# Near keys per block of 64 queries instead of 128, in an attention kernel on one NeuronCore

## The chip, the cores and the metric

The kernel runs on one core of a Trainium2 chip. The metric is the device time of one execution in microseconds; the numbers below are the median of three runs and one profiled execution. The engines are PE (TensorE, matmuls; PEld is its loading of weights), DVE (VectorE), ACT (ScalarE), POOL (GpSimd) and SP (SyncE, which here only issues DMAs).

## The reference

`x` is [4, 2048, 256] in float32. It is normalised over its last axis (xn), and the result is x plus an attention of xn plus a linear layer of xn with weights and activations rounded to fp8. The attention has 16 heads of 16 columns and a sparse mask:

```python
def _strided_allowed(S):                       # STRIDE = 4, LOCAL = 8
    i = jnp.arange(S)[:, None]
    j = jnp.arange(S)[None, :]
    return (j % STRIDE == 0) | (jnp.abs(i - j) <= LOCAL)
...
q = q * jax.nn.sigmoid(unity_scale)
scores = jnp.einsum('bhqd,bhkd->bhqk', q, k) / jnp.sqrt(jnp.asarray(D, x.dtype))
scores = jnp.where(allowed, scores, -jnp.inf)
attn = jax.nn.softmax(scores, axis=-1)
out = jnp.einsum('bhqk,bhkd->bhqd', attn, v)
out = out.transpose(0, 2, 1, 3).reshape(B, S, H)
return out @ o_w + o_b
```

So each query sees every fourth key of the sequence (512 "far" keys, the same for all queries) and the keys within 8 places of it ("near" keys, of which only those not divisible by 4 are still missing).

## The kernel before, in words

The first part (part_project) normalises x, computes q, k, v and the linear layer, splits q and k into parts in float16 and writes q, k, v to DRAM. The change touches it only where v is written: `v_sb` has 17 columns a head, the last of them 1, which gives the sum of the softmax.

The second part (part_attend) has 64 steps: 4 batches x 4 groups of 4 heads (16 iterations) x 4 blocks of 512 queries. The four heads of a group are two pairs (p = 0, 1); the two heads of a pair (f = 0, 1) lie in the two halves of the partitions of `q_op` and `k_op`, 48 rows each (51 with the negated maximum), so that the two matmuls of a pair can run side by side in two halves of the array's rows.

Each step does three things, and each for another step of the sequence:

- Maxima. For the next step and the one after it, PE computes the scores with queries in the partitions (`unit`): eight far units (128 queries x 512 far keys x 2 heads, L1105) and two near units (two tiles of 128 queries each, 108 near keys a tile: a mask matmul L1116 and the products L1123). Each unit fills one of two buffers of two PSUM banks (`ps_u`), and one DVE reduction (L1012, L1015) empties it. When the maxima of a step are complete, DVE joins them (L995, `maximum`, after AHEAD = 5 units), POOL splits the result into three parts in bf16 (L819 to L825), PE transposes it (L1061, `score_peaks`), ACT copies it (L946) and SP copies it into three rows of `q_op` (L859), where the far and near scores of the next step subtract it.
- Scores of the step itself, with keys in the partitions: `score_far` (L1070, 128 far keys x 512 queries, two heads, two banks; 8 pairs a step) and `score_near` (a mask matmul L1080 and a product L1083 for each tile of 128 queries, 108 keys a tile; 2 pairs of banks a step). ACT takes the exponential of each bank (L953 far, L958 near) into `probs`. There are three banks for scores (`ps_s`); `free_score` waits for the entry three before.
- The weighing (`weigh`): four rounds of far keys (L1142, four heads in four quarters of the array's columns, f32, 512 queries) and one of near keys (L1149, the same in tiles of 128 queries), all into one bank `ps_o`. ACT copies it out (L937) after the last round; DVE inverts the sums (L988), POOL multiplies (L810), SP stores.

Each engine's order is written out by hand. PE's is in `body(st)` of `tensor_attend`, ACT's in SCORE_PAIRS, DVE's in MAXIMA. PE's step before is:

```python
far_unit(2, 1); far(0, 0); weigh_last(2); far(0, 1); far_unit(1, 0); far_unit(0, 0)
far(2, 1); weigh_last(3); far(1, 0); near_unit(0); far_unit(2, 0); far(1, 1)
weigh_last(4); near(0); far_unit(3, 1); far_unit(1, 1); far(2, 0); weigh_own(0)
maxima(); far(3, 1); far_unit(3, 0); near_unit(1); far(3, 0); weigh_own(1)
near(1); far_unit(0, 1)
```

SP's order in a step: the shares of the step before to DRAM (L883), q of three steps ahead (L100), one piece of the next iteration's k or v (`load_piece` 0), the shares back, broadcast (L895), the attention rows out (L899), the sums (L851), the second piece (`load_piece` 1), the negmax rows (L859). The pieces of places 0 and 1 are k, those of places 2 and 3 are v: one DMA of far v (`r` = -1) and three of near v (L844, 36 rows x 16 tiles of 272 bytes each).

A third part multiplies with `o_w` and adds (L1222, L1031).

Of the kernel before, what the change touches and what calls it, by code (L numbers as in the profile page):

```python
# [22 lines left out]
BF16 = mybir.dt.bfloat16  # L23
F16 = mybir.dt.float16
I32 = mybir.dt.int32
ALU = mybir.AluOpType
# [19 lines left out]
HALF = P // 2  # L46
# [4 lines left out]
MASK_K = WPAD + S - NS + WPAD  # L51
# [7 lines left out]
VR = D + 1  # L59
EPS = 1e-5  # L60
BANDS = ((1, 18), (6, 6), (21, 5))
# [41 lines left out]
def part_project(nc, io, dram, keep, ctx):  # L103

    with ExitStack() as memory:
# [31 lines left out]
        v_sb = sb("v_sb", [P, 2, TT, NH, VR])  # L137
# [72 lines left out]
        def sync_project(sp):  # L210
# [13 lines left out]
            sp.dma_start(keep["mask_k"][:], io["near_k"].bitcast(BF16)).then_inc(keep["bands_loaded"], 16)  # L224
            sp.dma_start(keep["mask_q"][:], io["near_q"].bitcast(BF16)).then_inc(keep["bands_loaded"], 16)
# [53 lines left out]
        def gpsimd_project(pool):  # L279
# [5 lines left out]
            nc.gpsimd.memset(v_sb[:, 0, :, :, D:VR], 1.0).then_inc(v_set, 1)  # L285
            nc.gpsimd.memset(v_sb[:, 1, :, :, D:VR], 1.0).then_inc(v_set, 1)
# [23 lines left out]
        def scalar_project(act):  # L310
# [6 lines left out]
            def body(j, n):  # L317
# [27 lines left out]
                if main:  # L345
# [7 lines left out]
                    if not (isinstance(c, int) and c < 2):  # L353
                        act.wait_ge(v_stored[k], 16 * earlier(j, n))
                    nc.scalar.activation(
                        v_sb[:, k].rearrange("p t h w -> p (t h) w")[:, :, 0:D],
                        ps_v.rearrange("p a (t w) -> p (a t) w", w=D), ACT.Copy).then_inc(v_copied, 1)
# [267 lines left out]
UNITS = TT * PAIRS + TT // 2  # L625
# [3 lines left out]
AHEAD = 5  # L629
# [5 lines left out]
    ("near", 0), ("far", 2, 0), ("negmax",), ("far", 3, 1), ("far", 3, 0),  # L635
    ("near", 1),
# [3 lines left out]
    ("far", 2, 1), ("far", 1, 0), ("far", 0, 0), ("near", 0), ("far", 2, 0),  # L640
    ("far", 3, 1), ("far", 1, 1), ("far", 3, 0), ("near", 1), ("far", 0, 1),
# [17 lines left out]
def part_attend(nc, io, dram, keep, out, ctx, done):  # L659
# [69 lines left out]
    k_op, mask_k, mask_q = keep["k_op"], keep["mask_k"], keep["mask_q"]  # L729
    v_op = [keep["v_op"], sb("v_op1", [P, NS // P + S // P, HG * VR])]  # L730
    probs = sb("probs", [P, ROUNDS, HG, CH])
# [53 lines left out]
    def window(p, tile):  # L785
        return p * S + WSTEP * tile
# [3 lines left out]

    def close(tile):
        return WSTEP * tile
# [39 lines left out]
    def sync_attend(sp):  # L832
        def load_v(it, par, windows=range(-1, STRIDE - 1)):

            v = dram["v"][it // G, :, it % G * HG * VR:(it % G + 1) * HG * VR]
            for r in windows:
                if r < 0:
                    to, src = v_op[par][:, 0:NS // P, :], v[LOCAL:LOCAL + S, :].rearrange(
                        "(c p r) w -> r p c w", p=P, r=STRIDE)[0]
                else:  # L840
# [73 lines left out]
        for k in range(2):  # L914
            sp.wait_ge(done["qk_stored"][k], 16 * 12 * B * CPB // 2)
            sp.wait_ge(done["v_stored"][k], 16 * B * CPB // 2)
        load_v(0, 0)
# [11 lines left out]
    def scalar_attend(act):  # L929
# [9 lines left out]
        def body(st):  # L939
            todo = st.entries()  # L940
            for kind in todo:
# [12 lines left out]
                else:  # L954
                    h = kind[1]
                    if kind in OPENS and st.n >= 1:
                        act.wait_ge(pv_done, ROUNDS * st.at())
                    ins = nc.scalar.activation(probs[0:WIN, ROUNDS - 1, h], ps_s[st.bank(kind)][0:WIN], ACT.Exp,  # L958
                                               scale=undo)
# [19 lines left out]
    def vector_attend(dve):  # L979

        def body(st):
# [16 lines left out]
            for i, kind in enumerate(MAXIMA):  # L998
# [14 lines left out]
                else:  # L1013
                    tile = 2 * kind[1]
                    ins = nc.vector.tensor_reduce(peak_near[:, :, tile:tile + 2].rearrange("q f t p -> q f (t p)"),  # L1015
                                                  banks[:, :, 0:2 * PAIRS * WIN].rearrange("q f (g w) -> q f g w",
                                                                                           w=WIN), AX_X, ALU.max)
# [26 lines left out]
    def tensor_attend(pe):  # L1044
# [27 lines left out]
        def score_near(st, p):  # L1072

            q, k = q_op[:, st.slot()], k_op[st.parity()]
            banks = [free_score(st, ("near", 2 * p + f)) for f in range(2)]
            for t in range(TT):
                tile = st.queries() * TT + t
                cols, at, at_mask = slice(t * P, (t + 1) * P), window(p, tile), close(tile)
                for f in range(2):
                    nc.tensor.matmul(banks[f][0:WIN, cols], mask_k[half(f), at_mask:at_mask + WIN],  # L1080
                                     mask_q[half(f), tile * P:(tile + 1) * P], start=True, stop=False)
                for f in range(2):
                    ins = nc.tensor.matmul(banks[f][0:WIN, cols], k[half(f, KM), at:at + WIN], q[half(f, KM), p, cols],  # L1083
                                           start=False, stop=True)
                    if t == TT - 1:
                        ins.then_inc(s_ready, 1)

        def unit(st, kind):
# [21 lines left out]
            for t in range(2):  # L1110
                tile = 2 * kind[1] + t
                cols = slice(tile * P, (tile + 1) * P)
# [248 lines left out]
```

## Time and profile before

| | |
|---|---|
| median of three runs | 1126.22 us (1123.71 to 1129.16) |
| span of the profiled execution | 1127.2 us, mean granted clock 0.986 |
| PE busy | 1070.1 us (95%) |
| DVE busy | 948.4 us (84%) |
| ACT busy | 811.9 us (72%) |
| POOL busy | 248.4 us (22%) |
| largest groups | L1012 DVE 608.7 us, L953 ACT 541.4 us, L1142 PE 270.2 us, L1070 PE 254.2 us, L1105 PE 187.9 us |

Busy time of an engine is the union of its instructions' intervals; matmuls overlap, and their ends are modelled, so PE's share is not its load. The rows of a timeline merge neighbouring instructions of one line: the first number is the start of the first, the second the time to the end of the last, and xN their count. The first 237 us or so are the projections, the last 60 us the output matmuls; between them lie the 64 steps.

### The profile page before, as it was taken

Reading aid. Unit: us, or ns where it says so; the run is one execution under the profiler, and the core shown is the slowest. Engines: PE = TensorE matmul, PEld = TensorE weight load, DVE = VectorE, ACT = ScalarE, POOL = GpSimd, SP = SyncE. Lnnn points to the kernel's source line nnn. Section 1 sums busy time; section 2 is a strip of 40 time slices with the busy share of each in tenths; the row PEclk is TensorE's granted clock in tenths of the full one; section 3 lists DMA queues with packets and bytes.
Section 4 is the critical chain, followed back from the end, with each engine's and each line's share of the span. In section 5 each row is a group of like instructions: output and inputs, shape, how many; then the busy total and the mean of one; then the engine's idle time right before and its main releaser. Section 6 shows DMA issues by size and latency. Waiting matters only on the chain.

```text
span 1127.2 us, 28640 instructions
## 1 busy us (share of the span) xinstructions
PE 1070.1 (95%) x10945; PEld 484.3 (43%) x10945; DVE 948.4 (84%) x1203; ACT 811.9 (72%) x1524; POOL 248.4 (22%) x381
## 2 busy tenths in 40 slices
PE   5899999969999999999999999999999999999898
PEld 3566666623333333333333333333333333333387
DVE  5888877588999999999999999999898999999133
ACT  2444344327988898888888888888898888888700
POOL 1433333301121212212121212212121212222100
PEclk9999999968999999999999999999999999999999
DMA  6566666641232333333332333333333333231167
GB/s 188 184 197 206 206 209 209 196 111 44 81 87 81 99 91 85 87 103 104 95 107 82 112 91 105 89 96 111 94 99 93 99 94 94 86 84 48 55 216 246
DMA packets 167066, 134.21 MB, mean 119 GB/s; under 512 B 70652, under 2 KB 146172, under 8 KB 166924
## 3 DMA queue, kind: packets, MB, share of 16 engines
q1 hardware_dynamic: 164344, 128.19, 38.4%
q10 hardware_dynamic: 2592, 4.26, 1.1%
q8 instruction: 85, 1.39, 0.5%
q14 instruction: 45, 0.37, 0.1%
HBM read 71.26 MB, written 59.84 MB: 116 GB/s over the span
## 4 chain that ended last, share of the span: by engine, by line
PE 74%; DVE 12%; issue 7%; DMA 5%; ACT 2%; SPq 0%; DVEq 0%; ACTq 0%
PE ps_attend L1142 15%; PE ps_attend L1070 11%; DVE peak_far L1012 10%; PE ps_attend L1105 9%; PE ps_attend L1149 5%; PE ps_attend L1222 5%; PE ps_project L607 5%; PE ps_project L597 5%; PE ps_project L576 4%; PE ps_attend L1080 4%; DMA sums<-out_rows 3%; PE ps_attend L1116 3%; PE ps_project L540 2%; PE ps_attend L1083 2%; PE ps_attend L1123 2%
## 5 line engine op out<-in xcount | busy, mean ns | idle before, releaser
L1012 DVE TENSOR_REDUCE peak_far<-ps_attend 128x2 f32<-128x1024 f32 x512 | 608.7, 1221 | 42.7 <-PE ps_attend L1105 31.3
L953 ACT ACTIVATE probs<-ps_attend 128x512 f32<-128x512 f32 x1024 | 541.4, 598 | 49.4 <-PE ps_attend L1070 46.2
L1142 PE MATMUL ps_attend<-probs,v_op 128*17 128x512 f32 x2048 | 270.2, 600 | 0.0
L1070 PE MATMUL ps_attend<-q_op,k_op 51*128 51x512 f16 x1024 | 254.2, 387 | 4.9 <-ACT probs L953 3.3
L1105 PE MATMUL ps_attend<-k_op,q_op 48*128 48x512 f16 x1024 | 187.9, 388 | 25.7 <-DVE peak_far L1012 15.3
L958 ACT ACTIVATE probs<-ps_attend 108x512 f32<-108x512 f32 x256 | 138.9, 594 | 35.7 <-PE ps_attend L1083 35.7
L1070 PEld LDWEIGHTS ps_attend<-q_op,k_op 51*128 51x128 f16 x1024 | 76.8, 93 | 195.6 <-ACT probs L953 137.4
L819 POOL CAST negmax<-peak 128x16 bf16<-128x16 f32 x64 | 12.7, 198 | 612.8 <-DVE peak L995 612.8
L1015 DVE TENSOR_REDUCE peak_near<-ps_attend 128x8 f32<-128x864 f32 x128 | 131.0, 1023 | 10.5 <-PE ps_attend L1123 10.4
L810 POOL TENSOR_TENSOR out_rows<-out_rows,share_rows 128x512 f32<-128x512 f32 x64 | 81.4, 1272 | 65.4 <-DMA share_rows<-shares_dram 63.0
L1105 PEld LDWEIGHTS ps_attend<-k_op,q_op 48*128 48x128 f16 x1024 | 49.7, 94 | 98.6 <-DVE peak_far L1012 71.6
L1080 PEld LDWEIGHTS ps_attend<-mask_q,mask_k 48*108 48x108 bf16 x1024 | 60.0, 125 | 69.4 <-ACT probs L953 56.1
L1080 PE MATMUL ps_attend<-mask_q,mask_k 48*108 48x128 bf16 x1024 | 78.7, 228 | 0.8 <-ACT probs L953 0.8
L1083 PE MATMUL ps_attend<-q_op,k_op 51*108 51x128 f16 x1024 | 73.6, 218 | 0.0
L1149 PE MATMUL ps_attend<-probs,v_op 108*17 108x128 f32 x2048 | 68.3, 274 | 0.0
L328 ACT ACTIVATE qk_parts<-ps_project,ranges 128x1024 f16<-128x1024 f32 x16 | 17.8, 1114 | 68.6 <-PE ps_project L576 62.0
L297 POOL TENSOR_TENSOR quant<-quant,power 128x1024 f32<-128x1024 f32 x16 | 37.7, 2357 | 116.9 <-DVE qk_parts L436 80.3
L1116 PE MATMUL ps_attend<-mask_k,mask_q 48*128 48x216 bf16 x512 | 59.0, 260 | 4.1 <-DVE peak_far L1012 1.6
L1083 PEld LDWEIGHTS ps_attend<-q_op,k_op 51*108 51x108 f16 x1024 | 61.5, 126 | 0.0
L576 PE MATMUL ps_project<-xnT,wq 128*128 128x512 f32 x128 | 60.2, 614 | 1.2 <-ACT xnT L335 1.2
L1142 PEld LDWEIGHTS ps_attend<-probs,v_op 128*17 128x17 f32 x2048 | 34.0, 95 | 59.3 <-issue 58.6
L1123 PE MATMUL ps_attend<-k_op,q_op 48*128 48x108 f16 x1024 | 58.4, 210 | 0.0
(82 smaller groups left out, 1037.9 us busy)
## 6 DMA issues: line engine op xcount, KB each, us to landing
share_rows<-shares_dram SPq DMA_DIRECT2D x64, 256.0 KB
attn_dram<-out_rows SPq DMA_DIRECT2D x64, 256.0 KB, 5.5
q_dram<-qk_parts SPq DMA_DIRECT2D x96, 128.0 KB
k_dram<-qk_parts SPq DMA_DIRECT2D x96, 128.0 KB
q_op<-q_dram SPq DMA_DIRECT2D x128, 96.0 KB, 2.4
k_op<-k_dram SPq DMA_DIRECT2D x64, 144.0 KB, 3.1
v_dram<-v_sb SPq DMA_DIRECT2D x16, 544.0 KB, 5.1
base<-in_x SPq DMA_DIRECT2D x16, 512.0 KB, 5.2
```

Of the source, the lines that this page charges most:

```text
L576: last = nc.tensor.matmul(ps_q[:, m], wq[:, i, m * P:(m + 1) * P], xnT[:, k, i], start=(i == 0), stop=(i == KC - 1))
L953: ins = nc.scalar.activation(probs[:, r, h], ps_s[st.bank(kind)], ACT.Exp, scale=undo)
L958: ins = nc.scalar.activation(probs[0:WIN, ROUNDS - 1, h], ps_s[st.bank(kind)][0:WIN], ACT.Exp, scale=undo)
L1012: ins = nc.vector.tensor_reduce(peak_far[:, :, p, tile], banks, AX_X, ALU.max)
L1015: ins = nc.vector.tensor_reduce(peak_near[:, :, tile:tile + 2].rearrange("q f t p -> q f (t p)"), banks[:, :, 0:2 * PAIRS * WIN].rearrange ...
L1070: nc.tensor.matmul(bank, k[half(f, KM), keys], q[half(f, KM), p], start=True, stop=True).then_inc(s_ready, 1)
L1080: nc.tensor.matmul(banks[f][0:WIN, cols], mask_k[half(f), at_mask:at_mask + WIN], mask_q[half(f), tile * P:(tile + 1) * P], start=True, st ...
L1083: ins = nc.tensor.matmul(banks[f][0:WIN, cols], k[half(f, KM), at:at + WIN], q[half(f, KM), p, cols], start=False, stop=True)
L1105: nc.tensor.matmul(banks[f], q[half(f), p, tile * P:(tile + 1) * P], k[half(f), strided(p):strided(p) + NS], start=True, stop=True).then_i ...
L1116: nc.tensor.matmul(banks[f][:, whole].rearrange("q (p w) -> q p w", p=PAIRS), mask_q[half(f), st.queries(d) * CH + tile * P:st.queries(d) ...
L1142: ins = nc.tensor.matmul(ps_o[h * VW:h * VW + VR], v[:, r, h * VR:(h + 1) * VR], probs[:, r, h], start=(r == 0), stop=False)
L1149: ins = nc.tensor.matmul(ps_o[h * VW:h * VW + VR, t * P:(t + 1) * P], v[0:WIN, tile, h * VR:(h + 1) * VR], probs[0:WIN, r, h, t * P:(t + 1 ...
```

## The change

The near keys are taken per 64 queries instead of 128. WIN, the near keys of a tile, falls from 108 to 60 and there are 32 tiles of them instead of 16 along the sequence.

- Near scores: the two heads of a pair now share one bank. Head f has its 60 keys in partitions 64 f to 64 f + 59, NEAR = 124 rows in all, and its matmuls use a quarter of the array (its half of the rows, its half of the columns). Both pairs are done at one place, `near()`: one mask matmul of 512 columns a pair, then 8 tiles x 2 heads of 64 columns for each pair. ACT has two near exponentials a step instead of four.
- The mask: a window of 60 keys against 64 queries is the same for all tiles, so the masks are matmuls of 62 rows with an identity, read from one tensor `masks` for whole banks; two extra rows hide the keys ahead of the sequence and behind it.
- Near units: one a step instead of two. Two tiles of 64 queries lie in the two halves of the partitions; one mask matmul of 480 columns a head, then 32 products of 60 columns (4 tiles of 128 queries x 2 pairs x 2 halves x 2 heads), each on a quarter of the array. DVE has one near reduction a step, of 960 columns.
- Weighing of the near keys: v is laid out block-diagonal (`v_near`, with zeros between), so one matmul weighs both heads of a pair: 124 rows of keys, 49 columns of weights, 64 queries; 16 of them a step. The columns of v of a pair are interleaved (`v_order` on the host, `columns_of`), so the weights are read with a step of two. `probs_near` has two buffers.
- v's loading: near v in two DMAs (f = 0, 1) for each of the three r, of 20 x 32 pieces of 136 bytes. `v_near` is set to zero by POOL at the start.
- PE's step in nine slots, each with one unit ahead of one pair of scores; AHEAD falls to 3, `maxima()` comes ahead of `near()`.

```diff
-WIN = (P + 2 * LOCAL) // STRIDE * (STRIDE - 1)
-WSTEP = P // STRIDE * (STRIDE - 1)
+HALF = P // 2
+NT = S // HALF
+WIN = (HALF + 2 * LOCAL) // STRIDE * (STRIDE - 1)
+WSTEP = HALF // STRIDE * (STRIDE - 1)
+NEAR = HALF + WIN
+MASK_ROWS = WIN + 2
+VP = 2 * VR
+VT = 2 * VW + VP
+VM = VW + VR
...
-UNITS = TT * PAIRS + TT // 2
+UNITS = TT * PAIRS + 1
-AHEAD = 5
+AHEAD = 3
...
 SCORE_PAIRS = (
     ("far", 0, 0), ("far", 0, 1), ("far", 2, 1), ("far", 1, 0), ("far", 1, 1),
-    ("near", 0), ("far", 2, 0), ("negmax",), ("far", 3, 1), ("far", 3, 0),
-    ("near", 1),
+    ("negmax",), ("near", 0), ("far", 2, 0), ("far", 3, 1), ("far", 3, 0),
 )
...
-                    to = v_op[par][r:WIN:STRIDE - 1, NS // P:, :]
-                    src = bass.AP(tensor=v.tensor, offset=v.offset + (1 + r) * NH * VR,
-                                  ap=[[STRIDE * NH * VR, WIN // 3], [P * NH * VR, S // P], [1, HG * VR]])
-                sp.dma_start(to, src).then_inc(v_loaded[par], 16)
+                for f in range(2):
+                    to = v_near[par][f * HALF + r:f * HALF + WIN:STRIDE - 1, :, f * 2 * VW:f * 2 * VW + VP]
+                    src = bass.AP(tensor=v.tensor, offset=v.offset + (1 + r) * NH * VR + f * VP,
+                                  ap=[[STRIDE * NH * VR, WIN // 3], [HALF * NH * VR, NT], [1, VP]])
+                    sp.dma_start(to, src).then_inc(v_loaded[par], 16)
...
+        def score_near(st):
 
             q, k = q_op[:, st.slot()], k_op[st.parity()]
+            banks = [free_score(st, ("near", p)) for p in range(PAIRS)]
+            for p in range(PAIRS):
+                nc.tensor.matmul(banks[p][0:NEAR], masks[half(p, MASK_ROWS), MASK_KS],
+                                 masks[half(p, MASK_ROWS), shown(MASK_Q, HALF, st.queries())], start=True, stop=False)
+            for p in range(PAIRS):
+                for t in range(CH // HALF):
+                    cols, at = slice(t * HALF, (t + 1) * HALF), window(p, st.queries() * CH // HALF + t)
+                    for f in range(2):
+                        ins = nc.tensor.matmul(banks[p][half(f, WIN), cols], k[half(f, KM), at],
+                                               q[half(f, KM), p, cols], start=False, stop=(t == CH // HALF - 1))
+                ins.then_inc(s_ready, 1)
...
+            for f in range(2):
+                mask = masks[half(f, MASK_ROWS), shown(MASK_K, WIN, st.queries(d))]
+                nc.tensor.matmul(banks[f][:, 0:TT * PAIRS * WIN].rearrange("q (t p w) -> q t p w", t=TT, p=PAIRS),
+                                 masks[half(f, MASK_ROWS), MASK_QS],
+                                 mask.rearrange("r (t w) -> r t w", t=TT).unsqueeze(2).broadcast_to(
+                                     [MASK_ROWS, TT, PAIRS, WIN]), start=True, stop=False)
+            for t in range(TT):
                 for p in range(PAIRS):
+                    for u in range(2):
+                        tile = 2 * t + u
+                        at = window(p, st.queries(d) * CH // HALF + tile)
+                        for f in range(2):
+                            ins = nc.tensor.matmul(
+                                banks[f][half(u, HALF), (t * PAIRS + p) * WIN:(t * PAIRS + p + 1) * WIN],
+                                q[half(f), p, tile * HALF:(tile + 1) * HALF], k[half(f), at],
+                                start=False, stop=(t == TT - 1 and p == PAIRS - 1))
...
+                for t in range(CH // HALF):
+                    tile, cols = st.queries(d) * CH // HALF + t, slice(t * HALF, (t + 1) * HALF)
+                    for p in range(PAIRS):
+                        ins = nc.tensor.matmul(ps_o[half(p, VM), cols], near[0:NEAR, tile, p:p + 2 * VM - 1:2],
+                                               probs_near[0:NEAR, (st.n + d) % 2, p, cols],
+                                               start=False, stop=(t == CH // HALF - 1))
...
             far_unit(2, 1)
             far(0, 0)
             weigh_last(2)
+            far_unit(1, 0)
             far(0, 1)
-            far_unit(1, 0)
             far_unit(0, 0)
             far(2, 1)
             weigh_last(3)
+            near_unit()
             far(1, 0)
-            near_unit(0)
             far_unit(2, 0)
             far(1, 1)
             weigh_last(4)
-            near(0)
             far_unit(3, 1)
+            maxima()
+            near()
             far_unit(1, 1)
             far(2, 0)
             weigh_own(0)
-            maxima()
+            far_unit(3, 0)
             far(3, 1)
-            far_unit(3, 0)
-            near_unit(1)
+            far_unit(0, 1)
             far(3, 0)
             weigh_own(1)
-            near(1)
-            far_unit(0, 1)
```

## Rows read from the trace of the kernel before

**Rows 1.** One line's instructions (L995) in the stretch 300 to 1100 us: durations, starts.
```profile
L995 DVE TENSOR_TENSOR peak<-peak_far,peak_near x59: 174/176/177, 308.4 to 1047.2; 128x16 f32<-128x16 f32 x59
```

**Rows 2.** Windows: stretch, its length, busy us of each engine, clock, DMA, GB/s.
```profile
core 0: us, PE busy (x) PEld busy (x) DVE busy (x) ACT busy (x) POOL busy (x), PEclk, DMA share, GB/s
653.49:666.11 12.62, 12.39 (x158) 4.63 (x154) 11.83 (x13) 11.24 (x23) 2.09 (x6) 1.00 0.31 89
```

**Rows 3.** Timeline of one step: start us, us, engine, instruction, count.
```profile
653.49 0.23 PE L1061 MATMUL ps_attend<-ident_bf,negmax 128*128 128x128 bf16 x1
653.65 0.39 PE L1070 MATMUL ps_attend<-q_op,k_op 51*128 51x512 f16 x2
...
655.04 1.05 PE L1142 MATMUL ps_attend<-probs,v_op 128*17 128x512 f32 x8
...
656.02 0.26 PE L1080 MATMUL ps_attend<-mask_q,mask_k 48*108 48x128 bf16 x2
...
657.06 0.70 PE L1070 MATMUL ps_attend<-q_op,k_op 51*128 51x512 f16 x2
...
657.70 1.05 PE L1142 MATMUL ps_attend<-probs,v_op 128*17 128x512 f32 x8
...
658.68 0.39 PE L1070 MATMUL ps_attend<-q_op,k_op 51*128 51x512 f16 x2
...
659.11 2.09 ACT L953 ACTIVATE probs<-ps_attend 128x512 f32<-128x512 f32 x4 [0.32 <-PE ps_attend L1070]
...
660.07 1.05 PE L1142 MATMUL ps_attend<-probs,v_op 128*17 128x512 f32 x8
...
661.06 0.39 PE L1070 MATMUL ps_attend<-q_op,k_op 51*128 51x512 f16 x2
...
662.45 1.07 PE L1149 MATMUL ps_attend<-probs,v_op 108*17 108x128 f32 x32
...
663.45 0.26 PE L1080 MATMUL ps_attend<-mask_q,mask_k 48*108 48x128 bf16 x2
...
663.59 0.60 ACT L937 ACTIVATE out_rows<-ps_attend 128x512 f32<-128x512 f32 x1
...
664.15 1.08 ACT L958 ACTIVATE probs<-ps_attend 108x512 f32<-108x512 f32 x2
...
665.12 1.05 PE L1142 MATMUL ps_attend<-probs,v_op 128*17 128x512 f32 x8
...
666.11 0.23 PE L1061 MATMUL ps_attend<-ident_bf,negmax 128*128 128x128 bf16 x1
```

**Rows 4.** Timeline, the step before that one: a far pair and its weighing.
```profile
644.76 0.38 PE L1070 MATMUL ps_attend<-q_op,k_op 51*128 51x512 f16 x2
645.07 1.05 PE L1142 MATMUL ps_attend<-probs,v_op 128*17 128x512 f32 x8
```

**Rows 5.** Timeline of the step of rows 3: inside the near unit and near scores.
```profile
661.38 0.26 PE L1123 MATMUL ps_attend<-k_op,q_op 48*128 48x108 f16 x4
661.48 0.26 PE L1116 MATMUL ps_attend<-mask_k,mask_q 48*128 48x216 bf16 x2
...
663.90 0.22 PE L1083 MATMUL ps_attend<-q_op,k_op 51*108 51x128 f16 x2
```

**Rows 6.** Groups by line and form: count, busy us, mean ns of one, idle before.
```profile
L953 ACT ACTIVATE probs<-ps_attend 128x512 f32<-128x512 f32 x1024 | 541.4, 598 | 49.4 <-PE ps_attend L1070 46.2
L1015 DVE TENSOR_REDUCE peak_near<-ps_attend 128x8 f32<-128x864 f32 x128 | 131.0, 1023 | 10.5 <-PE ps_attend L1123 10.4
L1149 PEld LDWEIGHTS ps_attend<-probs,v_op 108*17 108x17 f32 x2048 | 50.5, 97 | 15.7 <-issue 13.7 <-ACT probs L953 1.7 <-ACT probs L958 0.3
L1222 PEld LDWEIGHTS ps_attend<-wo,heads 128*128 128x128 f32 x240 | 45.5, 190 | 7.2 <-issue 1.1
```

**Rows 7.** Timeline, SP's queue: one near v load, then the negmax rows.
```profile
652.23 0.82 SPq L844 DMA_DIRECT2D v_op<-v_dram  x1
...
654.05 1.54 SPq L859 DMA_DIRECT2D q_op<-negmax_rows  x2
```

More of the change, by code:

```diff
@@ L785, in window, with columns_of, shown @@
     def window(p, tile):
-        return p * S + WSTEP * tile
+        at = p * S + WSTEP * tile
+        return slice(at, at + WIN)
+    def columns_of(r, h, n):
+        first = (r * 2 + h % 2) * VP + h // 2
+        return slice(first, first + 2 * n - 1, 2)
+    def shown(columns, tile, queries):
+        first = columns.start + (0 if queries == 0 else 2 if queries == CPB - 1 else 1) * tile
+        return slice(first, first + columns.stop - columns.start - 2 * tile)
     def strided(p):
         return WPAD + p * S + S - NS
-    def close(tile):
-        return WSTEP * tile
     def gpsimd_attend(pool):
@@ L954, in body @@
                 else:
[L955 to L959, printed above, removed]
+                    if kind in OPENS and st.n >= 2:
+                        act.wait_ge(pv_done, ROUNDS * st.at(-1))
+                    ins = nc.scalar.activation(probs_near[0:NEAR, st.n % 2, kind[1]], ps_s[st.bank(kind)][0:NEAR],
+                                               ACT.Exp, scale=undo)
                 ins.then_inc(s_used, 1)
@@ L1132, in weigh @@
+        def weigh(st, d, r):
+            far, near = v_far[st.parity(d)], v_near[st.parity(d)]
             if r == 0:
                 if st.queries(d) == 0:
-                    pe.wait_ge(v_loaded[st.parity(d)], 64 * (st.half_iteration(d) + 1))
+                    pe.wait_ge(v_loaded[st.parity(d)], 16 * 7 * (st.half_iteration(d) + 1))
                 if st.n + d >= 1:
@@ L1158, in far_unit, with near_unit @@
                 unit(st, ("far", tile, p))
-            def near_unit(tiles):
-                unit(st, ("near", tiles))
+            def near_unit():
+                unit(st, ("near",))
             def far(r, p):
@@ L1268, in build @@
             "k_op": [sb(f"k_op{i}", [P, SK], F16) for i in range(2)],
-            "v_op": sb("v_op0", [P, NS // P + S // P, HG * VR]),
-            "mask_k": sb("mask_k", [P, MASK_K], BF16),
-            "mask_q": sb("mask_q", [P, S], BF16),
+            "v_far": [sb(f"v_far{i}", [P, NS // P * HG * VR]) for i in range(2)],
+            "v_near": [sb(f"v_near{i}", [P, NT, VT]) for i in range(2)],
+            "masks": sb("masks", [P, MASKS], BF16),
             "undo": sb("undo", [P, 1]),
@@ L1321 @@
     from concourse.bass_utils import run_bass_kernel_spmd
-    place = np.arange(-WPAD, S - NS + WPAD)
-    rows = np.concatenate([np.arange(n)[:, None] == place // size % n for size, n in BANDS])
-    close = np.abs(STRIDE * (place // 3) + 1 + place % 3 - np.arange(S)[:, None]) <= LOCAL
-    near_q = np.zeros((2, HALF, S), np.float32)
-    near_q[:, :len(rows)] = np.where(rows.astype(int) @ close.T.astype(int), 0, -BIG)
-    near_k = np.zeros((2, HALF, MASK_K), np.float32)
-    near_k[:, :len(rows)] = rows
-    near_k[:, :len(rows), :WPAD] = near_k[:, :len(rows), -WPAD:] = 1
+    key = np.arange(WIN)
+    apart = np.abs(STRIDE * (key // 3) + 1 + key % 3 - LOCAL - np.arange(HALF)[:, None]).T > LOCAL
+    masks = np.zeros((2, HALF, MASKS), np.float32)
+    masks[:, :WIN, MASK_Q] = np.tile(np.where(apart, -BIG, 0), CH // HALF + 2)
+    masks[:, :WIN, MASK_QS] = np.tile(np.where(apart, -BIG, 0), 2)
+    masks[:, :WIN, MASK_K] = np.tile(np.eye(WIN), TT + 2)
+    masks[:, :WIN, MASK_KS.start:MASK_KS.start + WIN] = masks[:, :WIN, MASK_KS.stop - WIN:MASK_KS.stop] = np.eye(WIN)
+    masks[:, WIN, MASK_Q.start:MASK_Q.start + HALF] = masks[:, WIN + 1, MASK_Q.stop - HALF:MASK_Q.stop] = -BIG
+    masks[:, WIN, MASK_QS.start:MASK_QS.start + HALF] = masks[:, WIN + 1, MASK_QS.stop - HALF:MASK_QS.stop] = -BIG
+    masks[:, WIN, MASK_K.start:MASK_K.start + WPAD] = masks[:, WIN + 1, MASK_K.stop - WPAD:MASK_K.stop] = 1
+    for f in range(2):
+        at = MASK_KS.start + f * HALF
+        masks[:, WIN, at:at + WPAD] = masks[:, WIN + 1, at + WIN - WPAD:at + WIN] = 1
+    v_order = [(g * HG + 2 * p + f) * D + i for g in range(G) for f in range(2) for i in range(D) for p in range(PAIRS)]
     def bf16_bits(a):
```

112 lines of the change are left out of this document (38 added, 74 removed).

## The prediction

> **What bounds the kernel now.** I first looked for the repeating unit. The maximum of all maxima (L995) runs once in each of the 64 steps; its first and last start in the stretch are 58 steps and 738.8 us apart, so a step takes 12.74 us [rows 1]. Then I read the busy time of one undisturbed step: 12.62 us long, with PE 12.39, DVE 11.83 and ACT 11.24 us busy at the full clock [rows 2]. A busy PE includes waits between overlapping matmuls, and DVE idles 0.79 us, so no engine's work alone makes the 12.62. What does is an order of waits, read from the timeline of one step [rows 3]: the reader should look at the start times of the PE rows and at the two ACT rows between them.
>
> Call N the negmax matmul (L1061), F a pair of far scores (L1070), W a weighing (L1142, or L1149 for the near keys), U a far unit (L1105), NU a near unit, "near" the near scores of one pair of heads (L1080). Start to start the step is: N to F 0.16; F to W 1.39; W to near 0.98; near to W 1.68 (F(0,0) at 657.06 in it); W to F 0.98; F to W 1.39; W to F 0.99; F to W 1.39; W(near) to near 1.00; near to W 1.67; W to N 0.99. The sum is 12.62 us: this one chain is the whole step. Three times F to W is 1.39, though the matmuls between need less. The reason is in F 658.68 and ACT 659.11: an exponential starts 0.43 us after F begins and is 0.60 long [rows 6], there are three score banks, and the second matmul of the next F needs the bank of this F's first. With 0.05 for the signals that is 1.08 us, and W starts 0.31 us behind. PE is in order, hence **an F that no W follows holds the chain 1.39 us, and units written inside that gap are free**. Today both near units and most far units lie in such gaps or in the near stations. An F whose two banks are both free costs only 0.31 us to its W [rows 4].
>
> **The change, walked through the same chain.** The nine slots: U F W / U F / U F W / NU F / U F W / U N near / U F W / U F / U F W. A unit now stands ahead of each F, so behind a W, where nothing hides it. Known pieces: W to the next start 0.98; a U ahead of an F 0.22 (512 columns at 2.4 GHz are 0.213); F to W 0.31 with free banks, 1.39 over a gap.
>
> Crossings: where PE goes from one shape of matmul to another the trace has 0.10 us over the stream: N is 128 columns, 0.053 us, and F follows it after 0.16 [rows 3]. The new near matmuls use half the array's columns (outputs at partitions 0 and 64) and their masks all, so NU and near each get a crossing inside and one behind. The trace has no such pair of shapes; bounds 0 and 0.10, and I take 0.10, since every pair of shapes there shows it.
>
> NU: two masks of 480 columns (0.20), a crossing, 32 products of 60 columns, a crossing. Today four products of 108 columns go in 0.10 us, and pairs of 128 columns 0.06 apart (seven of them from 663.45 to 663.90) [rows 3, 5], 5 to 10 ns over the stream. The new products fall on four quarters of the array and could run four at once: 8 groups at 0.045 (0.025 of stream, the overhead, and some of the loads, which a stream this short may not hide) make 0.36. So NU is 0.20 + 0.10 + 0.36 + 0.10 = 0.76 us. Bounds: without crossings and at 0.028 a group 0.42; and, at the pace of the densest long run of the trace, W(near), 32 matmuls in 1.00 less a crossing [rows 3] or 28 ns each, 0.20 + 0.10 + 0.90 + 0.10 = 1.30.
>
> near: mask 0.22, crossing 0.10, the first bank's 8 pairs of 64 columns at 0.04, so 0.28 to the start of the last; the exponential 0.25 later (663.90 to 664.15 [rows 3, 5]), 0.65 until its bank is free, 0.31 to W: 1.81 us. Bounds 1.63 (no crossing, 0.028 a pair) and 1.95 (28 ns a matmul). This one station replaces two (1.68 and 1.67). The rest of what ACT saves (two exponentials a step) is off the chain.
>
> W(near): 16 matmuls of 128 columns, four at once, become 16 of 64, two at once: the same stream; the f32 weights have 49 columns, not 17. Loads hide today; they take 97 ns for 17 columns and 190 for 128 [rows 6], so by the difference 41 ns for 49 columns beside the fixed part. I take 1.03 us; bounds 1.00 and 1.40 (all 32 loads in a row, 1.31, and a crossing).
>
> The sum from W to W: W, U, F 0.98 + 0.22 + 0.31 = 1.51; W, U, F, gap 0.98 + 0.22 + 1.39 = 2.59; W, NU, F, gap 0.98 + 0.76 + 1.39 = 3.13; W(near), U with its crossing, N, near 1.03 + 0.31 + 0.16 + 1.81 = 3.31; W, U, F, gap 2.59. **Step 13.13 us against 12.62**, +0.51. One near station of 1.68 goes; against it stand the NU outside the gaps (0.76) and four U that no gap hides.
>
> Off the chain. DVE: one near reduction of 960 columns, some 1.13 by the 1.02 of 864 [rows 6], in place of two; 11.83 - 2.04 + 1.13 = 10.9 us, over 2 us of slack. Nine units at 1.2 each against a walk of 1.46 each; only two pairs of units are 0.44 apart, with over 1.4 on both sides, so the two buffers cover it. POOL's negmax chain starts two units earlier. ACT: each exponential in a gap still finds ACT idle. SP: the near v goes out in six DMAs per iteration, not three (3 x 576 pieces of 272 B become 6 x 640 of 136 B), each 0.82 us of SP's time [rows 7]. Behind v on SP is queued the negmax copy into q_op, for which the next step's F(0,0) waits. Today it is issued at 654.05 and F(0,0) starts at 657.06, 3.01 us later [rows 3, 7]. In the walk SP has the sums and two v issues (0.82 each at most) after the out_rows copy (which starts 1.14 after W(near) and takes 0.60), so 4.2 us after W(near) starts, and F(0,0) comes at 7.1: 2.9 us. The cover just holds: 0. Without it each late v issue costs 0.8 in a step. The memsets of v_near, the one mask load and three more v loads at the start lie beside longer work: 0, bounds 0 and +2.5 us in all.
>
> The total is 64 x 0.51 = +33 us. The profiled execution spans 1127.2 us, 1.0 over the median of the runs; the steps' +33 go on the median: 1126.2 + 33 = 1159 us. What disturbs steps today (12.74 less 12.62, 0.12 each) is left as it is.
>
> **Weighed against the Trainium skill.** The trace's densest long run has 28 ns a matmul, with 128 columns each [rows 3]. The page "TensorE: Matmul & The Clock Gate" (section "Wait — 56ns, not 53.3ns?") says that start to start never falls below about 25 ns however few the columns. By it NU's products would take 0.80, not 0.36, and near's first bank 0.38, not 0.28: 13.67 us a step and 1193 us, an estimate from that page. It is nearly rival 1. Today each row tile of the near scores has its bank; the new kernel puts both heads into one. The page "TensorEngine Tiling (Array Packing)" (Gotcha 1: PSUM Pressure) says that different row tiles can't access one PSUM bank at once; by it the first bank's pairs would run apart, at most rival 1's pace there, +0.14 us a step. No row shows either yet.
>
> **Rivals.** (1) PE's rate binds. Small matmuls go at 28 ns each as in W(near): NU 1.30, near to W 1.95, a step of 13.81, +1.19 x 64 = +76: 1202 us. For it: no stretch is denser for long. Against it: that stretch is as long as its columns ask. (2) DVE bounds. It has the highest net work, and the change takes 0.91 from it; if the step followed with the same idle time it would be 11.7, -58: 1068 us. Against it: the chain gives the step to 0.01 us without DVE. It decides only if the 1.39 gaps shrink when ACT has less to do, and in the undisturbed rows ACT isn't behind there. (3) No crossings and quick pairs: NU 0.42, near to W 1.63, W(near) 1.00: 12.58, 1124 us, and 1116 if today's disturbances go too. (4) The negmax copy comes late behind v's doubled DMAs: +0.8 in half the steps on top of the forecast: 1185. That the change does less than it says has no room: a near unit and two near exponentials are gone from the loops.
>
> **How the numbers follow.** Forecast 1159: 0.55; rival 1: 0.20; rival 2: 0.10; rival 3: 0.10, half of it within 0.5%; rival 4: 0.05. Within 0.5% is about what a measurement of this kernel can't tell from no change. So faster 0.15, slower 0.80, same 0.05. The range takes in rivals 1 and 4 and the upper part of rival 3; it leaves out rival 2 and W(near) at its far bound on top of the rest: 1120 to 1205.
>
> **What would show it.** Steps of 13.1 us by L995; F to W 1.39 in four gaps; behind each W a unit after 0.98 and its F 0.22 later; NU to F 0.76 (1.3 is rival 1, 0.4 rival 3); near to W 1.8; DVE idle 2 us of each step. Wrong: a step near 11.7 with DVE without gaps (rival 2), or F(0,0) waiting for q_op's DMA (rival 4). The sum fails as a whole if PE gets the second matmul of an F earlier than 1.08 us after the pair before.

## The result and the profile after

The changed kernel takes 1149.55 us (median of 4 runs, 1148.81 to 1153.19), the kernel before 1126.45 (median of 4). The ratio is 1.022, with a 95% interval of 1.019 to 1.024: slower by 23 us, about 2%. The forecast was 1159 us, slower by 33.

The page of the changed kernel, its first line and its PE clock. DVE and ACT are busy for less time than before and PE for the same, and the kernel is slower:

```profile
PE 1069.8 (93%) x11713; PEld 460.0 (40%) x11713; DVE 899.3 (78%) x1139; ACT 738.2 (64%) x1396; POOL 254.0 (22%) x383
...
PEclk9999999969999999999999999999999999999999
```

DVE lost 49 us and ACT 74 us of busy time, PE nothing, and the clock is what it was (mean 0.988, before 0.986). So the 23 us don't show in any engine's busy time. For PE that alone says little, since its busy time includes waits between overlapping matmuls and it has 768 more of them (11713, before 10945); where its time goes is read from the step. The line of the step, as [rows 1]: L1013 is the maximum of all maxima now.

```profile
L1013 DVE TENSOR_TENSOR peak<-peak_far,peak_near x59: 174/176/178, 308.0 to 1070.7; 128x16 f32<-128x16 f32 x59
```

762.7 us over 58 steps are 13.15 us a step; before it was 12.74. The 58 steps hold 762.7 - 738.8 = 23.9 us of the 24.2 by which the profiled spans differ (1151.4 and 1127.2). What lies ahead of the first mark ends at 308.0 and before at 308.4. Nearly the whole loss is in the steps.

An undisturbed step of the changed kernel is 13.10 us, 667.01 to 680.12. Its timeline answers to [rows 3]: the columns are start, length, engine, instruction, count, and in brackets the idle time ahead and what ended it. L1078 is N, L1094 and L1100 are the near scores' masks and products, L1087 is F, L1121 U, L1128 and L1138 the near unit, L1159 W, L1166 W(near).

```profile
667.01 0.23 PE L1078 MATMUL ps_attend<-ident_bf,negmax 128*128 128x128 bf16 x1
667.17 0.43 PE L1094 MATMUL ps_attend<-masks 62*124 62x512 bf16 x2
...
667.53 0.66 PE L1100 MATMUL ps_attend<-q_op,k_op 51*60 51x64 f16 x32
...
668.13 0.39 PE L1121 MATMUL ps_attend<-k_op,q_op 48*128 48x512 f16 x2
...
668.97 1.07 PE L1159 MATMUL ps_attend<-probs,v_far 128*32 128x512 f32 x8
...
669.97 0.39 PE L1121 MATMUL ps_attend<-k_op,q_op 48*128 48x512 f16 x2
670.19 0.38 PE L1087 MATMUL ps_attend<-q_op,k_op 51*128 51x512 f16 x2
...
671.26 0.39 PE L1087 MATMUL ps_attend<-q_op,k_op 51*128 51x512 f16 x1 [0.25 <-ACT probs L972]
671.58 1.05 PE L1159 MATMUL ps_attend<-probs,v_far 128*17 128x512 f32 x8
...
672.56 0.39 PE L1121 MATMUL ps_attend<-k_op,q_op 48*128 48x512 f16 x2
...
672.79 0.38 PE L1087 MATMUL ps_attend<-q_op,k_op 51*128 51x512 f16 x2
673.10 1.06 PE L1159 MATMUL ps_attend<-probs,v_far 128*17 128x512 f32 x8
...
674.32 0.38 PE L1087 MATMUL ps_attend<-q_op,k_op 51*128 51x512 f16 x2
...
675.70 1.05 PE L1159 MATMUL ps_attend<-probs,v_far 128*17 128x512 f32 x8
...
676.69 0.38 PE L1128 MATMUL ps_attend<-masks 62*128 62x480 bf16 x2
676.99 0.44 PE L1138 MATMUL ps_attend<-k_op,q_op 48*64 48x60 f16 x32
...
677.37 0.39 PE L1087 MATMUL ps_attend<-q_op,k_op 51*128 51x512 f16 x2
...
678.76 1.11 PE L1166 MATMUL ps_attend<-probs_near,v_near 124*49 124x64 f32 x32
679.80 0.39 PE L1121 MATMUL ps_attend<-k_op,q_op 48*128 48x512 f16 x2
...
680.12 0.23 PE L1078 MATMUL ps_attend<-ident_bf,negmax 128*128 128x128 bf16 x1
```

What to see: three times F to W is 1.39 us with one unit inside (670.19, 674.32, 677.37). In the first of these gaps the second matmul of the next F starts at 671.26, 1.07 after the F that opened the gap. Before, these gaps held two units or a near unit and a far one. Now four far units (669.97, 672.56, 679.80 and the one at 674.09, left out above) and the near unit (676.69, 0.68 us until the F) stand behind a W, where they add to the step.

Two windows, the first a step of the changed kernel as [rows 2] is one of before (length, then the busy time of each engine):

```profile
600.69:613.79 13.10, 12.34 (x167) 4.24 (x166) 11.06 (x11) 10.10 (x21) 2.09 (x5) 1.00 0.40 99
679.90:693.00 13.10, 12.35 (x167) 4.25 (x165) 11.05 (x12) 10.10 (x20) 3.63 (x6) 1.00 0.33 96
```

DVE is busy 11.06 of 13.10 us, ACT 10.10. Both fell (from 11.83 and 11.24), and the step grew by 0.48 us.

### The profile page after: what moved, and what is told of

Its sections match the earlier page's. It is cut to its first block, busy times and chain, and to the rows that moved or that the text cites. A ratio compares the mean times of both kernels' runs of the same rounds, so it can differ in the third digit from the quotient of the medians.

```text
span 1151.4 us, 29905 instructions
## 1 busy us (share of the span) xinstructions
PE 1069.8 (93%) x11713; PEld 460.0 (40%) x11713; DVE 899.3 (78%) x1139; ACT 738.2 (64%) x1396; POOL 254.0 (22%) x383
## 4 chain that ended last, share of the span: by engine, by line
PE 82%; ACT 10%; DVE 2%; DMA 2%; issue 1%; SPq 1%; DVEq 0%; ACTq 0%
PE ps_attend L1159 21%; PE ps_attend L1087 15%; ACT probs L972 10%; PE ps_attend L1121 8%; PE ps_attend L1166 6%; PE ps_project L605 5%; PE ps_attend L1235 5%; PE ps_project L615 4%; PE ps_project L584 4%; PE ps_attend L1100 3%; PE ps_project L548 2%; PE ps_attend L1138 2%; PE ps_attend L1094 2%; PE ps_attend L1128 2%; PE ps_project L594 1%
## 5 line engine op out<-in xcount | busy, mean ns | idle before, releaser
L1087 PE MATMUL ps_attend<-q_op,k_op 51*128 51x512 f16 x1024 | 289.6, 384 | 51.7 <-ACT probs L972 49.6
L1159 PE MATMUL ps_attend<-probs,v_far 128*17 128x512 f32 (+1 forms) x2048 | 270.9, 602 | 0.0
L1121 PE MATMUL ps_attend<-k_op,q_op 48*128 48x512 f16 x1024 | 200.8, 388 | 8.1 <-DVE peak_far L1030 6.1
L1087 PEld LDWEIGHTS ps_attend<-q_op,k_op 51*128 51x128 f16 x1024 | 73.3, 94 | 203.1 <-ACT probs L972 149.6
L1121 PEld LDWEIGHTS ps_attend<-k_op,q_op 48*128 48x128 f16 x1024 | 49.5, 94 | 196.8 <-DVE peak_far L1030 128.3
L1032 DVE TENSOR_REDUCE peak_near<-ps_attend 128x16 f32<-128x960 f32 x64 | 74.1, 1158 | 28.7 <-PE ps_attend L1138 27.7
L976 ACT ACTIVATE probs_near<-ps_attend 124x512 f32<-124x512 f32 x128 | 69.5, 594 | 28.4 <-PE ps_attend L1100 28.3
L1166 PE MATMUL ps_attend<-probs_near,v_near 124*49 124x64 f32 x2048 | 70.7, 222 | 0.0
L1166 PEld LDWEIGHTS ps_attend<-probs_near,v_near 124*49 124x49 f32 x2048 | 61.3, 125 | 15.1 <-issue 15.1
L1159 PEld LDWEIGHTS ps_attend<-probs,v_far 128*17 128x17 f32 (+1 forms) x2048 | 36.2, 100 | 69.2 <-issue 46.4
L605 PE MATMUL ps_project<-xnT,wk 128*128 128x512 f32 x128 | 59.3, 607 | 0.0
L615 PE MATMUL ps_project<-wv,xnT 128*128 128x256 f32 x256 | 57.9, 379 | 0.0
L615 PEld LDWEIGHTS ps_project<-wv,xnT 128*128 128x128 f32 x256 | 48.6, 190 | 13.4 <-issue 7.6
L1235 PE MATMUL ps_attend<-wo,heads 128*128 128x256 f32 x240 | 52.0, 379 | 0.8 <-ACT out_rows L956 0.8
L1235 PEld LDWEIGHTS ps_attend<-wo,heads 128*128 128x128 f32 x240 | 45.5, 190 | 7.1 <-issue 0.9
```

Source lines behind the costliest of these rows:

```text
L605: last = nc.tensor.matmul(ps_k[:, m], wk[:, i, m * P:(m + 1) * P], xnT[:, k, i], start=(i == 0), stop=(i == KC - 1))
L615: last = nc.tensor.matmul(ps_v[:, t // 2, t % 2 * H:(t % 2 + 1) * H], xnT[:, k, i, t * P:(t + 1) * P], wv[:, i], start=(i == 0), stop=(i = ...
L1032: ins = nc.vector.tensor_reduce(peak_near[:].rearrange("q f t p -> q f (t p)"), banks[:, :, 0:TT * PAIRS * WIN].rearrange("q f (g w) -> q ...
L1087: nc.tensor.matmul(bank, k[half(f, KM), keys], q[half(f, KM), p], start=True, stop=True).then_inc(s_ready, 1)
L1121: nc.tensor.matmul(banks[f], q[half(f), p, tile * P:(tile + 1) * P], k[half(f), strided(p):strided(p) + NS], start=True, stop=True).then_i ...
L1159: ins = nc.tensor.matmul(ps_o[h * VW:h * VW + n], far[:, columns_of(r, h, n)], probs[:, r, h], start=(r == 0), stop=False)
```

## Experiments

Two theories ahead of the runs. **Chain**: the step is a sum of waits in PE's order. An F that no W follows holds PE until an exponential has freed its bank, 1.39 us to the next W; units in that gap are free and units behind a W are not. So the order makes the kernel slower, and the new data layout by itself would make it faster. **New matmuls**: the crossings between array shapes and the 68 small matmuls of the near unit and near scores cost the time, wherever they stand. A third, DVE, is in the forecast as rival 2. Of the first four kernels, e1 has the new layout with the units in the gaps and e2 the old layout with the units behind W: the two missing corners of layout and order. e3 and e4 each shorten one engine's instruction alone. The diffs of PE's order put several entries on a line. e2, e3, e4 and e6 are single runs; what is read from them is a difference of some 30 us or more, or the length of a step in the trace.

### e1: the new layout, units back in the gaps

```diff
             far_unit(2, 1); far(0, 0); weigh_last(2)
-            far_unit(1, 0); far(0, 1); far_unit(0, 0); far(2, 1); weigh_last(3)
-            near_unit(); far(1, 0); far_unit(2, 0); far(1, 1); weigh_last(4)
-            far_unit(3, 1); maxima(); near(); far_unit(1, 1); far(2, 0); weigh_own(0)
-            far_unit(3, 0); far(3, 1); far_unit(0, 1); far(3, 0); weigh_own(1)
+            far(0, 1); far_unit(1, 0); far_unit(0, 0); far(2, 1); weigh_last(3)
+            far(1, 0); near_unit(); far_unit(2, 0); far(1, 1); weigh_last(4)
+            maxima(); near(); far_unit(3, 1); far_unit(1, 1); far(2, 0); weigh_own(0)
+            far(3, 1); far_unit(3, 0); far_unit(0, 1); far(3, 0); weigh_own(1)
```

> The changed kernel with all its data layout, near unit, masks and block-diagonal v; only the order of TensorE's body(st) is different: the units stand in the gaps behind a far pair that no weighing follows, as in the kernel before (NU with far_unit(2,0) in one, two far units each in two others, far_unit(3,1) and far_unit(1,1) behind near()). Chain theory (a far pair without a weighing behind it holds PE 1.39 us to the next weighing, units in that gap are free, units behind a weighing are not): the near unit (0.68) and three or four far units (0.22 each) leave the path, against some 0.3 us of waiting for DVE where two units stand together; a step of 11.9 to 12.1 us instead of 13.10, and 1075 to 1090 us. Rival 'the new near matmuls cost it' (crossings between array shapes and 68 small matmuls are what makes the changed kernel slower, wherever they stand): 13.0 us or more, within 10 us of 1150. Rival DVE: no change, DVE's work is the same.

Measured: 1100.2 us (median of 4), ratio to before 0.976 (0.974 to 0.977). The order alone makes 49 us of difference to the changed kernel, with every matmul of it in place. "New matmuls" falls, and so does DVE as the bound of the changed kernel, since its work is the same here. The step, by the line of the maximum:

```profile
L1013 DVE TENSOR_TENSOR peak<-peak_far,peak_near x59: 174/176/178, 305.1 to 1022.1; 128x16 f32<-128x16 f32 x59
```

That is 12.36 us on average, while an undisturbed step is 12.09 (N at 650.64 and again at 662.73), as the chain said. The time is 10 us above the upper end of what was expected, because what disturbs the steps costs 0.27 us a step on average and not the 0.05 of the changed kernel. The waits of F in this kernel (line L1087, us and times in the stretch 300 to 1030, weight loads and matmuls added up) say by what; the copy of the negmax rows is the new one:

```profile
  ACT probs L972: 180.1, 240
  DMA q_op<-negmax_rows: 25.0, 24
  ACT probs_near L976: 11.8, 59
```

And within the undisturbed step the second unit of a gap now waits for DVE:

```profile
653.73 0.39 PE L1087 MATMUL ps_attend<-q_op,k_op 51*128 51x512 f16 x2
...
654.83 0.39 PE L1121 MATMUL ps_attend<-k_op,q_op 48*128 48x512 f16 x2 [0.49 <-DVE peak_far L1030]
655.06 0.38 PE L1087 MATMUL ps_attend<-q_op,k_op 51*128 51x512 f16 x2
655.37 1.05 PE L1159 MATMUL ps_attend<-probs,v_far 128*17 128x512 f32 x8
```

This gap is 1.64 us, not 1.39: 0.25 us of the gain go back to DVE, since a unit needs one of the two buffers that DVE empties. With a shorter chain the engine with the most work beside PE comes into it. A second wait is new too: N stands right behind a W now, the masks of the near scores find their bank still in use, and N to near is 0.29 us where it was 0.16:

```profile
650.64 0.23 PE L1078 MATMUL ps_attend<-ident_bf,negmax 128*128 128x128 bf16 x1
...
650.90 0.16 PEld L1094 LDWEIGHTS ps_attend<-masks 62*124 62x124 bf16 x2 [0.17 <-ACT probs L972]
650.93 0.43 PE L1094 MATMUL ps_attend<-masks 62*124 62x512 bf16 x2
```

### e2: the old layout, units behind the weighings

```diff
             far_unit(2, 1); far(0, 0); weigh_last(2)
-            far(0, 1); far_unit(1, 0); far_unit(0, 0); far(2, 1); weigh_last(3)
-            far(1, 0); near_unit(0); far_unit(2, 0); far(1, 1); weigh_last(4)
-            near(0); far_unit(3, 1); far_unit(1, 1); far(2, 0); weigh_own(0)
-            maxima(); far(3, 1); far_unit(3, 0); near_unit(1); far(3, 0); weigh_own(1)
-            near(1); far_unit(0, 1)
+            far_unit(1, 0); far(0, 1); far_unit(0, 0); far(2, 1); weigh_last(3)
+            near_unit(0); far(1, 0); far_unit(2, 0); far(1, 1); weigh_last(4)
+            far_unit(3, 1); near(0); far_unit(1, 1); far(2, 0); weigh_own(0)
+            maxima(); far_unit(3, 0); far(3, 1); near_unit(1); far(3, 0); weigh_own(1)
+            far_unit(0, 1); near(1)
```

> The kernel before, unchanged but for TensorE's order, in which now each unit stands behind a weighing as in the changed kernel (ten units, two near ones). Chain theory: far_unit(1,0), near_unit(0), far_unit(3,1), far_unit(3,0) and far_unit(0,1) come onto the path, 4 x 0.22 + 0.39 = 1.27 us, so 13.89 us a step instead of 12.62 and about 1205 us. Rival 'the new near matmuls cost it': 12.62 and 1126, since none of them is in this kernel. Rival DVE: 1126, the same work.

Measured: 1195.1 us in the one run, 10 us under the expected 1205, and steps of 13.80 us (800.6 us over 58):

```profile
L995 DVE TENSOR_TENSOR peak<-peak_far,peak_near x59: 174/176/177, 312.1 to 1112.7; 128x16 f32<-128x16 f32 x59
```

The order alone costs the old layout 68 us. No step is disturbed: all 58 are 13.80 or 13.81 us long, and the DVE waits for the sums that the kernel before has (7.4 us in all, see below) are gone. With a longer chain whatever is late has time to come. The missing 0.09 us of the expected 13.89 are in the two near stations:

```profile
649.06 0.22 PE L1080 MATMUL ps_attend<-mask_q,mask_k 48*108 48x128 bf16 x2
649.11 0.22 PE L1083 MATMUL ps_attend<-q_op,k_op 51*108 51x128 f16 x2
...
650.68 1.05 PE L1142 MATMUL ps_attend<-probs,v_op 128*17 128x512 f32 x8
```

near to W is 1.62 here and 1.68 in [rows 3]. Now a far unit stands ahead of the near scores, and not a weighing, and the first mask is followed by its product after 0.05 us (before 0.10, 656.02 to 656.12).

### e3: DVE's far reductions halved

```diff
-                    ins = nc.vector.tensor_reduce(peak_far[:, :, p, tile], banks, AX_X, ALU.max)
+                    ins = nc.vector.tensor_reduce(peak_far[:, :, p, tile], banks[:, :, 0:CH // 2], AX_X, ALU.max)
```

and `scale=0.0` in both exponentials.

> The changed kernel with each far maximum taken over 256 of the 512 keys a head (and all exponentials of zero, so that nothing overflows): the far keys' other half and the softmax's weights are left out. Only DVE's far reductions get shorter, 1.19 to about 0.65 us. Chain theory: DVE is not in it, 13.10 us a step and 1145 to 1151 us. Rival DVE: eight times 0.5 us less a step, so a step of 9 to 12.5 us and under 1115 us.

Measured: 1147.9 us in one run, undisturbed steps 13.11 us, the mean of the 58 is 13.13:

```profile
L1013 DVE TENSOR_TENSOR peak<-peak_far,peak_near x59: 174/176/177, 302.9 to 1064.3; 128x16 f32<-128x16 f32 x59
```

A far reduction went from 1.22 to 0.69 us, and the step didn't move. DVE isn't in the step of the changed kernel. Rival 2 falls.

### e4: ACT's far exponentials halved

```diff
-                    ins = nc.scalar.activation(probs[:, r, h], ps_s[st.bank(kind)], ACT.Exp, scale=undo)
+                    ins = nc.scalar.activation(probs[:, r, h, 0:CH // 2], ps_s[st.bank(kind)][:, 0:CH // 2], ACT.Exp, scale=undo)
```

with one memset of the other half of `probs` ahead of the steps.

> The changed kernel with each far exponential over 256 of the 512 queries (the other half of the weights is set to 1 once and left out afterwards). Only ACT's far exponentials get shorter, 0.60 to about 0.39 us. Chain theory: the gap from a far pair to the next pair's second matmul is 0.43 + the exponential + 0.05, so 0.87 instead of 1.08 us, in three gaps a step: 13.10 - 0.63 = 12.47 us a step and about 1110 us. Rival 'PE's own matmuls and crossings set the step': 13.10. Rival DVE: 13.10.

Measured: 1115.0 us in one run; the undisturbed step is 12.46 us (12.47 expected), the mean one 12.61, since F's weight loads wait for the negmax copy 19 times, 10.4 us. A far exponential took 0.384 us instead of 0.600. One gap of it in its timeline (here L1092 is F, L1126 U, L1166 W, L977 the exponential):

```profile
648.78 0.38 PE L1092 MATMUL ps_attend<-q_op,k_op 51*128 51x512 f16 x2
649.00 0.38 PE L1126 MATMUL ps_attend<-k_op,q_op 48*128 48x512 f16 x2
...
649.19 1.25 ACT L977 ACTIVATE probs<-ps_attend 128x256 f32<-128x256 f32 x4 [0.97 <-PE ps_attend L1092]
...
649.95 1.05 PE L1166 MATMUL ps_attend<-probs,v_far 128*17 128x512 f32 x8
```

F to W is 1.17 us instead of 1.39, although ACT sat idle for 0.97 us ahead of the first exponential. So what counts is not ACT's load but the length of one exponential, which sets how long a filled bank stays in use.

### e5: as e1, and the negmax copy ahead of the second piece on SP

```diff
-            load_piece(st, 1)
             if ("negmax",) in st.entries():
                 move_negmax(st)
+            load_piece(st, 1)
```

> The kernel of e1 (units in the gaps), and SP issues the copy of the negmax rows into q_op ahead of the second piece of k or v, not behind it. In e1 the undisturbed step is 12.09 us but the mean one 12.36, and far(0,0) waits for that copy 24 times, 25 us in all. Theory (the copy is queued on SP behind the sums and one or two v loads): those waits go, 25 us less whatever else is late next; mean step 12.10 to 12.20 us and 1084 to 1092 us. Rival (the copy is late on its own because the DMA engines are full with v's 136-byte pieces, in whatever order SP issues): within 5 us of e1's 1100. Bound on the other side: k and v land later, and if a step waits for them instead, no gain either.

Measured: 1089.0 us (median of 5, 1086.5 to 1089.4), ratio to before 0.966 (0.964 to 0.968). The mean step is 12.13 us (703.4 over 58), the undisturbed one still 12.09. The waits for the copy (us, times, longest) in e1 and then in this kernel, both between the first and last mark:

```profile
PEld ps_attend L1087 <- DMA q_op<-negmax_rows: 14.4, 14, 2.0
PE ps_attend L1087 <- DMA q_op<-negmax_rows: 10.3, 9, 1.7
```

```profile
PEld ps_attend L1087 <- DMA q_op<-negmax_rows: 1.5, 2, 1.1
PE ps_attend L1087 <- DMA q_op<-negmax_rows: 0.8, 1, 0.8
```

One wait can stand in both rows, for the load of the weights and for the matmul, so the first row is the nearer reading: 14.4 us became 1.5, and the 58 steps became 13.6 us shorter. It was the place in SP's queue and not the traffic: the bytes and pieces are the same. **This version beats both kernels**, the one before by 3.4% and the changed one by 61 us. The copy's queue hasn't been tried alone in the kernel before.

### e6: the near unit alone moved into a gap

```diff
-            near_unit()
             far(1, 0)
+            near_unit()
             far_unit(2, 0)
```

> The changed kernel with two neighbouring entries of TensorE's order swapped: near_unit() stands behind far(1,0) and not ahead of it, so in a gap; nothing else moves. Chain theory: the near unit's 0.68 us leave the path, but far(1,0) + near unit + far_unit(2,0) are 0.22 + 0.68 + 0.22 = 1.12 us and the gap holds 1.08, so 0.04 comes back: 13.10 - 0.64 = 12.46 us an undisturbed step, about 1110 us. Rival 'the new near matmuls cost it wherever they stand': 13.10. It also reads alone what of e1's gain is the near unit's place and what the far units'.

Measured: 1119.9 us in one run; the undisturbed step is 12.47 us (12.46 expected), the mean one 12.59 (730.1 over 58). The time lies 10 us above the expected one. Disturbed steps are 4 us of that (0.12 us a step on average, 0.05 in the changed kernel; F's weight loads wait for the negmax copy 11 times here, 8.0 us), and 3 us are the steps outside the marks: all that lies there got 0.7 us shorter, not six times 0.64. The rest is no more than runs of one kernel differ by (the changed kernel's from 1148.8 to 1153.2). One swap of two neighbouring lines is worth 0.63 us an undisturbed step, where 0.64 was counted. From e6 to e1, the places of three far units, it is another 0.38. Two of the units cost 0.22 each behind a W and the third 0.32 between W(near) and N, 0.76 in all; of that 0.25 go to DVE's wait and 0.13 to the wait behind N, both shown in e1.

The four corners, in us: old layout with the units in gaps 1126, old layout behind W 1195, new layout behind W 1150, new layout in gaps 1100. The layout gains 26 us in the one order and 45 us in the other; the order costs 49 or 68. "Layout" here is all of the change but the order; its parts were not tried one by one.

## Why the prediction was right, and where it was off

- **The chain as the bound.** This was right. The order moves the undisturbed step as the sum says (within 0.01 us in e6, within 0.09 in e2, inside the expected range in e1), the exponential's length sets the gap to 0.01 us (e4), and DVE's work doesn't enter in the changed kernel (e3).
- **Near unit.** 0.76 us forecast, 0.68 measured (676.69 to 677.37). Its 32 products with a crossing behind them take 0.38 us (676.99 to 677.37), so about 0.28 without, 0.035 for four and 9 ns for one. The trace has their single starts: groups of four 0.032 us apart (0.052 after the first), and about 3 ns between the four. I had taken 0.045 for four; four at once on four quarters was right.
- **Near scores.** near to W 1.81 forecast, 1.80 measured (667.17 to 668.97). The 32 products take 0.60 with the crossing behind them, 0.50 without: 0.03 a pair.
- **W(near).** 1.03 forecast, 1.04 measured (678.76 to 679.80). The 49-column f32 loads hide: 32 of them stand in that time, which was 1.00 before.
- **Crossings.** Mask to products is 0.36 us for 512 columns (0.213 of stream) and 0.30 for 480 (0.20): 0.10 to 0.14 over it, the taken value or a little more. That a crossing costs this is measured; whether it is the change of shape itself or a weight load that can't go ahead of it was not separated.
- **The sum.** 13.13 forecast, 13.10 measured. Of the 10 us between the forecast +33 and the measured +23, the size of the step is 2 (0.51 against 0.48), the disturbances are 4 and the count of steps 3, both below. The last 1 us lies between the profiled executions (24.2 us apart) and the medians (23.1). That the sum is so near is a little luck: it has 0.08 too much for the near unit and 0.01 or 0.02 too little at several other places.
- **The balance in words.** "One near station of 1.68 goes" against the near unit and four U doesn't give +0.51: 0.76 and 4 x 0.22 are 1.64. In the station's place stands F to W of 0.31, the other station grows by 0.13 and the U ahead of N has a crossing of 0.09 (with 0.01 from the weighings, and 1.67 for the station that goes). The list of the sum has them, the sentence doesn't.
- **Disturbances.** I left them as they were, 0.12 us a step, and gave no reason; they fell to 0.05, which is 4 us over 58 steps. Before, DVE waited in them for the sums' DMA, now it hardly does. The reciprocal comes later behind the sums' issue than before (4.2 us, 667.43 to 671.63; before 3.9, 651.59 to 655.53). e2, where the old layout has a longer step, has no such wait and no disturbed step at all, which fits. No kernel moved the reciprocal or the sums' issue alone, so the cause is argued and not shown:

```profile
DVE shares L988 <- DMA sums<-out_rows: 7.4, 8, 1.4
```

```profile
DVE shares L1006 <- DMA sums<-out_rows: 0.3, 1, 0.3
```

(the first of the kernel before, the second of the changed one, both between their first and last marks).

- **The count of steps.** I multiplied by 64. All that lies outside the marks, six steps among it, grew by 0.3 us together where I had 3 for those six. The slice of the page with the lower granted clock and the steps with units or scores missing lie there; what each contributes was not taken apart. With 58 steps of 0.41 us the 24 us come out.
- **Negmax copy.** "The cover just holds" was right for the changed kernel (six waits of the weight loads, 3.4 us) and shows as soon as the step gets shorter: 14.4 us of weight loads' waits in e1, of which moving the copy gave back 11 us of time (e5). It was rival 4's mechanism, in another kernel.
- **Rivals.** Rival 1, PE's rate of 28 ns a matmul, is out by the 9 ns above (the stretch with 28 ns had f32 matmuls of 128 columns), and with it, for this kernel, the 25 ns floor that the Trainium skill gives ("TensorE: Matmul & The Clock Gate", section "Wait — 56ns, not 53.3ns?"): the trace has nearly three times that rate where neighbours use different parts of the array. The rule on PSUM ("TensorEngine Tiling (Array Packing)", Gotcha 1) would have the two heads of a pair, in one bank now, run apart. The trace has 0.030 us from pair to pair and 2 ns between the two, and 0.027 us of stream for one, so here they run together; they write different partitions of the bank. Rival 2 fell with e3, rival 3 with the crossings.
- **A slip.** The last part speaks of "four gaps"; the sum has three, and the trace has three.

## What to carry to other kernels

When three engines are each about 90% busy or more in a step (here 89, 94 and 98%), look for a repeating unit and write out the start times of the in-order engine: if a short chain of differences adds up to the unit, the order of its instructions is the bound, and taking work from an engine that isn't in that chain gains nothing (here DVE, in e3), until the chain gets so short that this engine comes into it (DVE in e1). Then place independent work in the waits of the chain (behind the instruction whose buffer comes back late) and not behind the instructions that end them. When such a chain gets shorter, check every queue whose cover was "just enough"; here a copy behind two loads on the DMA-issuing engine took back 11 us.

## What the runs showed of the hardware

- Matmuls of 60 columns on four quarters of the array (64 rows by 64 columns each) start at a mean of 9 ns (four every 0.032 us), and those of 64 columns on two diagonal quarters, into one PSUM bank, at 15 ns (two every 0.030 us). The densest long run of the kernel before had 28 ns, with f32 matmuls of 128 columns.
- Where the array's shape changes, the next matmul starts 0.10 to 0.14 us later than the stream asks at the full clock: 0.16 us behind N with 0.053 of stream, 0.32 from a far unit to N with 0.213, and from masks on all columns to products on half of them 0.30 with 0.20 and 0.36 with 0.213. Between matmuls of one shape (U and F) it is 0.22 with 0.213.
- A far exponential over 256 columns instead of 512 (0.384 us, not 0.600) frees its bank 0.22 us earlier, and PE gets all of it back in each of three places (the step falls by 0.64 us), though ACT idles ahead of it.
- One small copy queued on SP behind one or two loads of k or v came late for 14.4 us of PE's weight loads in 58 steps; ahead of them, for 1.5 us, with the same bytes moved (e1, e5).
